# One-hot tables with the edge tile as the innermost index, read by TensorE with a step

## The reference

```python
x = x + gnn(layernorm(x), edge_index, edge_attr)      # two attention layers over the edges
x = x + ffn(layernorm(x))                             # eight experts, one for each node
x = x + hops(layernorm(x), edge_index)                # five times h = A_norm @ h, gated sum
x = x + slice_attention(layernorm(x))
```

## Time and the profile before

| | us |
|---|---|
| median of 3 runs | 2994.82 |
| lowest and highest run | 2990.13, 2995.47 |
| profiled execution, first to last instruction | 2989.7 |
| stage A, its DVE groups | about 20 to 115 |
| stage B, its windows | about 162 to 309 |
| stage C, layer 0 | about 502 to 670 |
| stage C, layer 1 | about 1150 to 1273 |

### The profile page before, as it was taken

How to read it: one execution, slowest core, us unless ns; L and a number is a source line. 1 busy time by engine, 2 the same in 40 slices (tenths; PEclk the granted TensorE clock), 3 DMA queues, 4 the chain that set the end, 5 groups by cost and what they waited for, 6 DMA issues and landing times. The chain is left out here.

```text
span 2989.7 us, 39776 instructions
## 1 busy us (share of the span) xinstructions
PE 2211.4 (74%) x11685; PEld 1650.5 (55%) x11685; DVE 1789.0 (60%) x4141; ACT 948.0 (32%) x1705; POOL 1059.9 (35%) x1034
## 2 busy tenths in 40 slices
PE   5469563517888653368887389928999999997977
PEld 1136452205666451145655367726888888886646
DVE  6488897756777495457775344447444444434753
ACT  5435100211222101100000022227766666664422
POOL 0000576756777476757777333030000000000000
PEclk9789786758999766689998599968999999998987
DMA  4144673334555364345565399733565555561001
GB/s 182 14 136 164 214 234 104 116 110 136 164 158 157 123 226 123 118 124 156 161 168 140 119 340 386 238 91 98 147 158 147 136 148 147 143 153 46 1 15 46
DMA packets 368926, 432.55 MB, mean 145 GB/s; under 512 B 48543, under 2 KB 322944, under 8 KB 365542
## 3 DMA queue, kind: packets, MB, share of 16 engines
q1 hardware_dynamic: 269610, 224.54, 25.4%
q0 software_dynamic: 50496, 151.74, 17.5%
q10 hardware_dynamic: 48656, 54.31, 5.5%
HBM read 333.58 MB, written 97.72 MB: 144 GB/s over the span
## 5 line engine op out<-in xcount | busy, mean ns | idle before, releaser
L2386 PE MATMUL hop_sums<-hop_pieces,hop_weights 128*128 128x512 f32 x3125 | 714.9, 391 | 65.4 <-DVE hop_pieces L2274 65.2
L2386 PEld LDWEIGHTS hop_sums<-hop_pieces,hop_weights 128*128 128x128 f32 x3125 | 589.8, 189 | 190.4 <-DVE hop_pieces L2274 66.9
L2323 ACT ACTIVATE hop_weights<-col_columns 128x640 fp32r<-128x640 f16 x625 | 458.7, 738 | 225.2 <-PE hop_sums L2386 202.9
L521 POOL DMA_INDIRECT gat_ring<-hx_rows,src_i x392 | 436.6, 1114 | 163.3 <-issue 118.4
L521 POOL DMA_INDIRECT gat_ring<-hx_next,src_i x392 | 388.3, 991 | 150.5 <-issue 115.0
L1813 PE MATMUL agg_acc<-gat_ring,agg_oh 128*128 x976 | 265.6, 416 | 66.9 <-DVE agg_oh L1714 64.2
L1813 PE MATMUL agg_acc<-agg_msg,agg_oh 128*128 x976 | 246.3, 402 | 51.5 <-DVE agg_oh L1717 51.4
L1813 PEld LDWEIGHTS agg_acc<-gat_ring,agg_oh 128*128 128x128 f32 x976 | 179.7, 200 | 147.5 <-issue 127.4
L2443 POOL IOTA slc_valid<- 128x25 f32 x1 | 0.2, 162 | 735.1 <-POOLq L76 735.1
L1714 DVE TENSOR_SCALAR agg_oh<-agg_nodes,dst_f,w_cols 128x128 f32<-128x128 f32 x488 | 174.9, 406 | 122.0 <-PE agg_acc L1813 67.8
L1813 PEld LDWEIGHTS agg_acc<-agg_msg,agg_oh 128*128 128x128 f32 x976 | 179.7, 195 | 111.5 <-issue 86.4
(11 more groups left out here) (466 smaller groups left out, 3036.1 us busy)
## 6 DMA issues: line engine op xcount, KB each, us to landing
col_columns<-count_rows SPq DMA_DIRECT2D x60, 1600.0 KB, 8.0
look_part<-src_low SPq DMA_DIRECT2D x28, 896.0 KB
exp_w<-in_L_ffn_w SPq DMA_DIRECT2D x16, 1024.0 KB, 10.2
count_windows<-cnt_out SPq DMA_DIRECT2D x67, 200.0 KB, 1.9
count_windows<-cnt_out ACTq DMA_DIRECT2D x64, 200.0 KB, 1.9
staged<-gat_ring ACTq DMA_DIRECT2D x14, 520.0 KB
gat_ring<-staged SPq DMA_DIRECT2D x14, 520.0 KB, 3.8
agg_res<-x_norm ACTq DMA_DIRECT2D x50, 128.0 KB, 3.5
```

Source lines behind the costliest of these rows:

```text
L521: pool.indirect_dma_start(out=self.ring[:, 4 * slot + 2 * (q % 2) + k, :], out_offset=None, in_=self.g.hx_rows, in_offset=bass.IndirectOff ...
L2323: act.activation(weights[:, q % SLOTS_W, :, :], columns[n % STAGES][:, c * GROUP:(c + 1) * GROUP, b % 2 * P:(b % 2 + 1) * P], ACT.Copy).th ...
L2386: mm = pe.matmul(sums[m % BANKS][:, :], weights[:, q % SLOTS_W, i, :], pieces[k % 2][:, t, :], start=(t == 0), stop=(t == NB - 1))
```

## The change

In both places the index of the tile moves from outside to innermost. A one-hot table that was [tile, number] becomes [number, tile], with 8 tiles in stage A and 4 in the windows. The row of numbers, which was read again for each tile, is written out once as `numbers`, each number 8 or 4 times; the digits of the tiles are read again for each number. PE now reads one tile's one-hot with a step of 8 or 4 elements, as weights and, in stage A, as moving columns too (`oh_high`). `src_hot` is unchanged.

```diff
@@ graph_tables
-        oh_low = s.sb("oh_low", [P, 2 * GRP, P], F16)
-        oh_high = s.sb("oh_high", [P, 2 * GRP, NB], F16)
+        numbers = s.sb("numbers", [P, P, GRP], F16)
+        oh_low = s.sb("oh_low", [P, 2, P, GRP], F16)
+        oh_high = s.sb("oh_high", [P, 2, NB, GRP], F16)
...
                 link(nc.vector.tensor_copy(count16[:, :], g.count[:, :]))
+                link(nc.vector.tensor_copy(numbers[:, :, :], count16[:, :].unsqueeze(2).to_broadcast([P, P, GRP])))
...
                     nc.vector.tensor_tensor(
-                        oh_low[:, half * GRP:(half + 1) * GRP, :], count16[:, :].unsqueeze(1).to_broadcast([P, GRP, P]),
-                        low[:, bass.ds(n * GRP, GRP)].unsqueeze(2).to_broadcast([P, GRP, P]), ALU.is_equal)
+                        oh_low[:, half, :, :], numbers[:, :, :],
+                        low[:, bass.ds(n * GRP, GRP)].unsqueeze(1).to_broadcast([P, P, GRP]), ALU.is_equal)
                     nc.vector.tensor_tensor(
-                        oh_high[:, half * GRP:(half + 1) * GRP, :],
-                        count16[:, 0:NB].unsqueeze(1).to_broadcast([P, GRP, NB]),
-                        high[:, bass.ds(n * GRP, GRP)].unsqueeze(2).to_broadcast([P, GRP, NB]),
+                        oh_high[:, half, :, :], numbers[:, 0:NB, :],
+                        high[:, bass.ds(n * GRP, GRP)].unsqueeze(1).to_broadcast([P, NB, GRP]),
                         ALU.is_equal).then_inc(hot, 1)
...
-                    for k in range(half * GRP, (half + 1) * GRP):
-                        mm = nc.tensor.matmul(hist[:, 0:NB], oh_low[:, k, :], oh_high[:, k, :],
+                    for k in range(GRP):
+                        mm = nc.tensor.matmul(hist[:, 0:NB], oh_low[:, half, :, k], oh_high[:, half, :, k],
                                               start=False, stop=False, skip_group_check=True)
@@ Counter
-    ... s.sb("dst_hot", [P, self.HOT, TRIPLE + 1, P], F16)
+    ... s.sb("dst_hot", [P, self.HOT, P, TRIPLE + 1], F16)
+        self.numbers = s.sb("numbers", [P, P, TRIPLE + 1], F16)
...
-            dve.tensor_tensor(self.dst_hot[:, j % self.HOT, 0:n, :], self.count16[:, :].unsqueeze(1).to_broadcast([P, n, P]),
-                              self.key[:, j, 0:n].unsqueeze(2).to_broadcast([P, n, P]), ALU.is_equal)
+            dve.tensor_tensor(self.dst_hot[:, j % self.HOT, :, 0:n], self.numbers[:, :, 0:n],
+                              self.key[:, j, 0:n].unsqueeze(1).to_broadcast([P, P, n]), ALU.is_equal)
...
-                    mm = pe.matmul(whole[j % sets][:, n, 0:self.COLS], self.dst_hot[:, j % self.HOT, i, :],
+                    mm = pe.matmul(whole[j % sets][:, n, 0:self.COLS], self.dst_hot[:, j % self.HOT, :, i],
@@ counts
                 link(dve.tensor_copy(c.count16[:, :], g.count[:, :]))
+                link(dve.tensor_copy(c.numbers[:, :, :], c.count16[:, :].unsqueeze(2).to_broadcast([P, P, TRIPLE + 1])))
```

More of the change, by code:

```diff
@@ L271, in _ @@
                 pe.wait_ge(hot, after(1))
-                nc.tensor.matmul(hist[:, 0:NB], zero16[:, :], oh_high[:, 0, :], start=True, stop=False,
+                nc.tensor.matmul(hist[:, 0:NB], zero16[:, :], oh_high[:, 0, :, 0], start=True, stop=False,
                                  skip_group_check=True)
@@ L288, in _ @@
                         done += 1
-                nc.tensor.matmul(hist[:, 0:NB], zero16[:, :], oh_high[:, 0, :], start=False, stop=True,
+                nc.tensor.matmul(hist[:, 0:NB], zero16[:, :], oh_high[:, 0, :, 0], start=False, stop=True,
                                  skip_group_check=True).then_inc(counted, 1)
@@ L690, in __init__ @@
         self.number, self.count16 = s.sb("number", [P, QUARTER], F16), s.sb("count16", [P, P], F16)
-        self.src_hot, self.dst_hot = s.sb("src_hot", [P, self.SRC, QUARTER], F16), s.sb("dst_hot", [P, self.HOT, TRIPLE + 1, P], F16)
+        self.src_hot, self.dst_hot = s.sb("src_hot", [P, self.SRC, QUARTER], F16), s.sb("dst_hot", [P, self.HOT, P, TRIPLE + 1], F16)
+        self.numbers = s.sb("numbers", [P, P, TRIPLE + 1], F16)
         self.out = s.sb("out", [P, self.OUT, QUARTER], F16)
```

## The result

| | before | after |
|---|---|---|
| median, us | 2993.21 (4 runs) | 2976.72 (4 runs) |
| lowest and highest run | 2990.13, 2995.47 | 2974.70, 2981.64 |
| profiled execution, span | 2989.7 | 2979.8 |

The ratio is 0.9947, 95% interval 0.9935 to 0.9960: 16 us faster, between 12 and 19. The profiled execution of the changed kernel is the slowest of its four runs (2981.64 with what lies around the span), so the profiles differ by 9.9 us only.

A forecast was written before the change was run, and what follows sets the result against it. Bounds differ by stage: PE-ACT loop in A, DVE then PE-ACT in B, POOL at DVE's period in C. Savings 0.6 + 4.1 + 12 = 16.7 us off 2989.7 give 2973.0, plus 5.1 for the median: 2978; range 2969 to 2992.

The forecast's parts named there:

- The forecast case: Whole kernel: savings in Stage A, Stage B and Stage C sum to 16.7 us, giving 2978 us; chance 0.60.
- The compare: One-hot compares reach two elements a cycle: 687, 419 and 256 ns for 1024, 512 and 200 elements.
- The rival that the rate doesn't come: Compares stay at one element a cycle: no effect but the copy, 2995 us; chance 0.09.
- Stage A: graph_tables: 31 us of DVE busy time saved, but only the first group's 0.64 us lies on the path.
- the sixth step: TensorE's strided reads of the one-hots: taken at no cost, with an upper bound of 14 us in Stage A.
- A's slack: PE's 0.4 + 0.94 us available for two groups in a round of Stage A, taken to cover strided loads.
- The copies: Writing out numbers: hidden under a 3.98 us wait in Stage A; 0.1 us taken in Stage B.
- Stage B: Counts: 3.2 us saved in windows 0 to 11, 1.0 at the end, less 0.1, together 4.1 us.
- Stage C: edge_weights: 46 POOL issues locked to DVE's window, 1.62 to 1.36 us, save 12 us; bounds 0 and 16.6.
- the third rival: The strided load costs what an fp32 one does: +14 us in Stage A, 2992 us; chance 0.07.
- The second rival: POOL's issues in Stage C miss their place and take two windows: net +13 us, 3008 us; chance 0.12.
- the first rival: POOL gains nothing in Stage C, as unchanged TENSOR_SCALARs do the blocking: −4.7 us, 2990 us; chance 0.12.

The follow-up runs named there:

- windows only: The changed kernel with graph_tables left as in the kernel before: 2979.26 us against 2993.97, ratio 0.9953.
- fours: The changed kernel with 4 tiles innermost in place of 8 in stage A's tables, a step of 8 bytes: 2975.92 us against 2994.29, ratio 0.9941.
- halves: The kernel called fours, with each src_hot compare of stage C in two of 400 elements: 2983.81 us against 2992.71, ratio 0.9966.
- three compares: The changed kernel with two more compares of 240 elements in each window of stage C: 2989.69 us, one run.
- tables only: Only graph_tables changed, the windows left as in the kernel before: 2995.29 us against 2993.97, ratio 1.0006.
- slow compare: The changed kernel, but in stage C the dst_hot compare reads its numbers with an innermost step of 0: 2988.15 us against 2993.97, ratio 0.9983.
- step alone: The new layouts everywhere, but all compares read their numbers with an innermost step of 0, as slow as before: 2991.86 us against 2993.97, ratio 0.9996.
- experiment 3: The same run as slow compare: the changed kernel with the old compare length in stage C, 2988.15 us, ratio 0.9983.
- experiments 9 to 11: Experiment 9, three compares and halves, which alter DVE's instructions in the windows of stage C: 3043.48, 2989.69 and 2983.81 us.
- experiment 9: The changed kernel, but in stage C the three src_hot compares of a window are TENSOR_TENSORs, no TENSOR_SCALAR left: 3043.48 us, one run.
- experiment 11: The same run as halves: src_hot compares of stage C split in two, on the kernel called fours, 2983.81 us, ratio 0.9966.
- experiment 8: The changed kernel with 70 matmuls of zeros on PE ahead of the first histogram group: 2978.27 us against 2994.29, ratio 0.9947.

## Why the prediction was right

The forecast case came (2978 forecast, 2976.7 measured), by its own mechanism; one term had the wrong sign and two were a little large. The range, 2969 to 2992, was wide enough to hold two of the rivals as well, so it is the stages that tell the forecast from them, and not the total.

1. *The compare* went at the pair rate as taken: 689 and 417 ns for 687 and 419, and `grf_oh_high` 255 for 256. The rival that the rate doesn't come fell.
2. *Stage A* was forecast at −0.6 and gave +1.5. The 0.6 came: the first `hidden` starts 0.59 us earlier. What failed is the sixth step, which set the stepped loads at nothing: they cost 2.1 us. "A's slack" was read from a late round, where it is there: fours 3.37 us apart, 0.34 left of 0.94. The first rounds have none. Before and after, PE's `hidden`:

```profile
25.85 1.88 PE L456 MATMUL grf_edge_ps<-grf_edge 32*128 32x448 f32 x8 [1.79 <-ACT grf_edge L444]
...
30.05 1.31 PE L456 MATMUL grf_edge_ps<-grf_edge 32*128 32x448 f32 x8
```

```profile
29.80 1.88 PE L457 MATMUL grf_edge_ps<-grf_edge 32*128 32x448 f32 x8
31.60 1.72 PE L465 MATMUL grf_edge_ps<-grf_edge 128*32 128x448 f32 x8
33.26 1.17 PE L280 MATMUL grf_hist<-grf_oh_high,grf_oh_low 128*128 128x25 f16 x16
34.35 1.88 PE L457 MATMUL grf_edge_ps<-grf_edge 32*128 32x448 f32 x8
...
38.56 1.03 PE L457 MATMUL grf_edge_ps<-grf_edge 32*128 32x448 f32 x8
```

At this slow pace a round is 1.88 + 1.72 + 1.17 us of PE, less the overlaps 34.35 − 29.80 = 4.55, without any wait: PE is the bound. Before, a slow round took 4.20 (30.05 − 25.85) with under 0.2 us to spare, so of the histogram's extra 0.56 us 0.35 count. A slow round costs 4.55 in place of 4.20, and there are more of them: always two with packed loads or steps of 8 bytes (before, windows only, fours, halves), three or four with steps of 16 bytes, in seven of the eight kernels that have them and start cold. The exception is the kernel with three compares (two slow rounds, and A −0.3). From a start 0.60 us earlier, the first `hidden` to the fifth: 38.56 − 21.05 = 17.51 us after, 37.07 − 21.64 = 15.43 before; 2.08 − 0.6 = 1.5.
3. *The copies* cost nothing that shows. In B the shift of the first window is that of the stage's start (+1.45 against +1.46): the wait of 0.52 us covered most of the 0.61, and one CAST beside it took 0.36 us where it had taken 0.55 in the profile before, which hides the 0.1 that was set.
4. *Stage B* gave 3.5 of 4.1. The shift went from +1.45 at window 0 to −1.64 at window 12: 3.1 of the 3.2 set. The pairs gave nothing, as forecast, and lost 0.3 between windows 12 and 60; the end gave 0.8 of the 1.0. The kernels whose clock stayed up at 185 to 190 us gave 3.7 to 3.9, so part of what is missing goes with TensorE's clock there; why it fell is open.
5. *Stage C* was set at 12 us of gain and gave 10.9 against the profile of before. Three kernels with the old period in C (tables only, slow compare, step alone) stand at +1.5 to +1.7 against that same profile, so against them it is 12.5. Layer 0 gave 6.3 (23 × 0.26 = 6.0 set), layer 1 4.6 (6.2 against those three). That the compare's length is the cause is shown by experiment 3. One issue to a window described before and after well, though its place in the window moved; as a general law it is too simple (experiments 9 to 11).
6. *The stepped reads*: free at a step of 8 bytes in the windows, as set; at 16 bytes in A not free. The load took 165 ns and the pitch was 0.063 us, a third of the way from 0.027 to 0.127. Sixteen of them are 1.0 us of the 1.34 available, so the third rival (+14 us) stayed away at the fast pace. The second rival, the missed place, didn't come in this kernel either: the issues took 1.06 us.

The Trainium skill, "SBUF — State Buffer", section "Who interferes with whom", stood behind the first rival: TENSOR_SCALARs can lock POOL out and a TENSOR_TENSOR takes only the read side, so unchanged TENSOR_SCALARs would keep their price. The runs don't bear it out here. With the same three TENSOR_SCALARs an issue takes 1.33 us beside a TENSOR_TENSOR of 0.67 and 1.06 beside one of 0.41 (experiment 3), and beside TENSOR_TENSORs alone issues of 1.49 us appear, and one of 43.16 (experiment 9). Its rule that either side may block the other does agree with experiment 11.

That the total came out within 1.3 us is partly luck, since it agrees better than its parts: A, B and C add up to −13.0 in the profile. That, the forecast's −16.7 and the measured ratio (−12 to −19) are compatible; the runs don't tell them apart.

*What stays open.* Why TensorE's clock rises later with steps of 16 bytes, and in one execution not; in the slow rounds PE is busier with them than without. And what inside a POOL issue waits for DVE, of which the runs show only the patterns.

## What to carry to other kernels

Before a compare is made faster, look at which other engine moves in step with it. Here 0.27 us off an instruction whose engine idles 15 us and more behind each batch was worth 11 to 12 us, because POOL's issues went at DVE's period, while 31 us of compares saved in stage A were worth the 0.6 us of the first group. A stepped weight load was free here at 113 ns under matmuls 0.169 us apart, and not under those 0.027 us apart. So check it against the smallest matmul and the slowest rounds of the stage, not against a late one, and prefer 8 bytes of step to 16.

## What the runs showed of the hardware

- A load of 128 × 128 fp16 weights took 96 to 98 ns packed, 113 to 118 with a step of 8 bytes, 165 with 16. Under 400-column matmuls 0.169 us apart the first step didn't show; under 25-column ones the pitch went from 0.027 to 0.035 and 0.063 us.
- TensorE starts stage A at a pace of 1.88 us for eight `hidden`, and later takes 1.03. With matmuls ahead of it (experiment 8) the rounds of 1.88 stand at a granted clock of 0.50 (1.2 GHz), those of 1.03 at 1.00 (2.4 GHz). Without them the column reads 1.00 at both paces, so in the first 30 to 38 us of these traces it is not to be trusted. In the changed kernel TensorE worked from 25.24 to 38.56 us without a wait, and its rounds were slow all that time. 70 matmuls ahead gave one fast round; in the wait of 1.22 us behind it the clock fell.
- POOL's indirect transfers, 0.94 to 0.97 us to issue alone, often fall into whole-number patterns with DVE's windows: one issue to a window of 1.36, 1.62 and 1.73 us, two to one of 3.07, three to two of 1.81 and 2.02. Not always: with three compares a batch went at 1.43 us in windows of 1.74. And the pattern of one kernel can differ from batch to batch: with halves, locked in one, and in the next POOL at its own 1.28 us with DVE held back.
- TENSOR_TENSORs alone can hold POOL: beside windows of four (3.04 to 3.07 us) every second issue took 1.49 us, and in one batch a single issue took 43.16 us, until DVE was through (experiment 9, one execution).
